# Graph attention on one core: ten of sixteen blocks of a tile turned by DMA instead of eight, with rows grouped by four tiles

## The reference

```python
h = maximum(layernorm(x, axis=-1), 0)             # x: 8192 x 128
scores = einsum('nd,md->nm', h, ks)               # ks: 8192 x 128, so 8192 x 8192 scores
scores = leaky_relu(scores, negative_slope=0.2)
scores = where(adj > 0, scores, -9e15)            # adj: 8192 x 8192 int32
attn = softmax(scores, axis=1)
out = x + einsum('nm,md->nd', attn, ks)
```

## Time and profile before

| | before |
|---|---|
| runs, us | 1636.68, 1636.82, 1636.87 |
| profiled execution, us | 1636.71 |
| its span, first to last instruction, us | 1634.9 |
| busy: PE, PEld, DVE, ACT, POOL | 98%, 72%, 89%, 86%, 71% |
| mean granted TensorE clock | 0.994 |
| HBM read, MB | 276.82 |

### The profile page before, as it was taken

How to read it: one execution, slowest core, us unless ns; L and a number is a source line. 1 busy time by engine, 2 the same in 40 slices (tenths; PEclk the granted TensorE clock), 3 DMA queues, 4 the chain that set the end, 5 groups by cost and what they waited for, 6 DMA issues and landing times.

```text
span 1634.9 us, 38135 instructions
## 1 busy us (share of the span) xinstructions
PE 1599.4 (98%) x13442; PEld 1183.9 (72%) x13442; DVE 1449.5 (89%) x2592; ACT 1401.3 (86%) x2081; POOL 1156.8 (71%) x1224
## 2 busy tenths in 40 slices
PE   5699999999999999999999999999999999999999
PEld 3377777777777777777777777777777777777777
DVE  7989898898898988988998988888898898898986
ACT  6688888888888888888888888888888888888887
POOL 1576776776777777777767777777777767767766
PEclk8999999999999999999999999999999999999999
DMA  7799999999999999999999999999999999999996
GB/s 236 189 232 267 262 269 252 256 274 261 256 266 254 263 266 263 258 261 263 260 271 255 260 271 253 268 266 256 266 265 252 272 261 256 268 254 261 277 256 125
DMA packets 641340, 417.78 MB, mean 256 GB/s; under 512 B 551040, under 2 KB 575616, under 8 KB 641152
## 3 DMA queue, kind: packets, MB, share of 16 engines
q1 hardware_dynamic: 641152, 415.34, 104.7%
HBM read 276.82 MB, written 4.19 MB: 172 GB/s over the span
## 4 chain that ended last, share of the span: by engine, by line
PE 93%; POOL 1%; DVE 0%; ACT 0%; DMA 0%; issue 0%; POOLq 0%; DVEq 0%
PE ps_out L386 26%; PE ps_scores L360 14%; PE ps_out L387 13%; PE ps_T L371 13%; PE ps_scores L362 13%; PE ps_scores L361 13%; POOL keys_in L314 0%; PE ps_out L338 0%; PE ps_out L385 0%; POOL keys_in L312 0%; PE ps_out L384 0%; DMA keys_in<-keys_in 0%; DVE keys L562 0%; DVE mask L573 0%; ACT scores L453 0%
## 5 line engine op out<-in xcount | busy, mean ns | idle before, releaser
L314 POOL TENSOR_TENSOR keys_in<-scores,keys_in 128x512 f16<-128x512 f32 x512 | 652.7, 1275 | 41.4
L591 DVE CUSTOM_DVE_ANT_0 scores<-ps_scores,mask,minus_scale 128x1024 f32<-128x1024 f32 x512 | 654.3, 1278 | 9.7 <-PE ps_scores L362 0.6
L312 POOL CAST keys_in<-scores 128x512 f16<-128x512 f32 x512 | 346.7, 677 | 379.2 <-ACT scores L462 378.9
L462 ACT ACTIVATE scores<-scores,neg_max 128x1024 f32<-128x1024 f32 x512 | 582.7, 1138 | 0.0
L453 ACT ACTIVATE scores<-scores 128x1024 f32<-128x1024 f32 x512 | 537.8, 1050 | 30.6 <-DVE pair_min L591 30.5
L600 DVE TENSOR_TENSOR probsT_lo<-ps_T,probsT_hi 128x512 f16<-128x512 f32 x512 | 352.0, 688 | 142.3 <-ACT probsT_hi L470 142.3
L470 ACT ACTIVATE probsT_hi<-ps_T 128x512 f16<-128x512 f32 x512 | 305.6, 597 | 184.7 <-PE ps_T L371 184.2
L360 PE MATMUL ps_scores<-keysT_hi,hT_hi 128*128 128x512 f16 x1024 | 391.4, 382 | 16.0 <-DVE keysT_lo L555 9.4
L386 PE MATMUL ps_out<-keys,probsT_hi 128*128 128x256 f16 x2048 | 393.6, 273 | 6.7 <-issue 6.0
L361 PE MATMUL ps_scores<-keysT_lo,hT_hi 128*128 128x512 f16 x1024 | 390.9, 382 | 0.0
L362 PE MATMUL ps_scores<-keysT_hi,hT_lo 128*128 128x512 f16 x1024 | 390.4, 381 | 0.0
(11 more groups left out here) (52 smaller groups left out, 831.5 us busy)
## 6 DMA issues: line engine op xcount, KB each, us to landing
adj_in<-in_adj_dram SPq DMA_DIRECT2D x512, 512.0 KB, 5.2
keys_in<-keys_in SPq DMA_TRANSPOSE x512, 5.1
x_in<-in_x_dram SPq DMA_DIRECT2D x64, 64.0 KB, 2.1
keys_in<-in_L_gnn_ks_dram SPq DMA_DIRECT2D x8, 512.0 KB, 7.3
out_dram<-out_tile SPq DMA_DIRECT2D x64, 64.0 KB, 1.8
```

What stands on the lines that cost most here:

```text
L312: nc.gpsimd.tensor_copy(half[:, 0:BLOCK], probs(t, b)).then_inc(half_hi_ready, 1)
L314: nc.gpsimd.tensor_tensor(half[:, BLOCK:2 * BLOCK], probs(t, b), half[:, 0:BLOCK], ALU.subtract) \
L462: nc.scalar.activation(s, s, ACT.Exp, bias=neg_max[:, t % 2:t % 2 + 1], scale=-SLOPE, accum_out=pair_sum[:, t % 2, p:p + 1]).then_inc(prob ...
L591: nc.vector.tensor_tensor_reduce(out=score_pair(q, p), in0=ps_scores[:, slots, :].rearrange("p s k -> p (s k)"), in1=mask[:, (p // 2) % 2, ...
```

## The change

`BY_DMA` gets blocks 4 and 12 as well, so ten blocks of a tile are turned by DMA and six by PE. The slots for halves become 6, for turned blocks 8. Adjacency gets a fourth buffer and is loaded six pairs ahead instead of four. The rows of a group of four tiles are dealt out so that partition p holds rows 4p to 4p+3 of the group: tile s of a group takes every fourth row. With that, one DMA of 256 KB loads `x` for four tiles and one stores four tiles of output, once in four steps; an adjacency row piece is still 4 KB, but the rows of neighbouring partitions lie 128 KB apart instead of 32 KB. On DVE, `split_h` moves from slot 14 to slot 13, ahead of slot 14's `split_probs_lo`, and a tile's first mask moves from slot 0 into slot 14 of the step before (the very first one to the front of the program).

```diff
-    ADJ_SLOTS = 3
+    ADJ_SLOTS = 4
...
-    R_SLOTS = 4
-    X_SLOTS = 4
-    D_SLOTS = 6
+    R_SLOTS = 6
+    GROUP = 4
+    GROUPS = TILES // GROUP
+    D_SLOTS = 8
...
-    BY_DMA = tuple(b for b in range(BLOCKS) if b % 2 == 1)
+    BY_DMA = tuple(b for b in range(BLOCKS) if b % 2 == 1 or b in (4, 12))
...
+        x_groups = x.rearrange("(g p s) d -> g p s d", p=P, s=GROUP)
+        out_groups = out.rearrange("(g p s) d -> g p s d", p=P, s=GROUP)
+        adj_tiles = adj.rearrange("(g p s) m -> g s p m", p=P, s=GROUP)
...
-            def store(t):
-                sp.wait_ge(out_ready, t + 1)
-                sp.dma_start(out[rows(t), :], out_tile[:, :]).then_inc(stored, 16)
+            def store(g):
+                sp.wait_ge(out_ready, (g + 1) * GROUP)
+                sp.dma_start(out_groups[g], out_tile[:, g % 2, :, :]).then_inc(stored, 16)
...
-            for p in range(4):
+            for p in range(6):
                 load_adj(0, p)
...
-                    if j == 11 and prev:
-                        store(i - 1)
-                    if j == 11 and i + 3 < TILES:
-                        load_x(i + 3)
+                    if j == 11 and prev and i % GROUP == 0:
+                        store(i // GROUP - 1)
+                        if i // GROUP + 1 < GROUPS:
+                            load_x(i // GROUP + 1)
...
             find_scales()
+            make_mask(0, 0)
             split_keysT_lo(0)
...
-                    if split and j == 0:
-                        split_probs_lo(*split)
-                    if more and j % 4 == 0:
+                    if more and j in (4, 8, 12):
                         make_mask(i + 1, j // 4)
...
-                    if split and j > 0:
+                    if ahead and j == 13:
+                        split_h(i + 2, odd)
+                    if split:
                         split_probs_lo(*split)
-                    if ahead:
-                        if j == 5:
-                            statistics(i + 2)
-                        if j == 14:
-                            split_h(i + 2, odd)
+                    if ahead and j == 14:
+                        make_mask(i + 2, 0)
+                    if ahead and j == 5:
+                        statistics(i + 2)
```

More of the change, by code:

```diff
@@ L88, in gat_kernel @@
         probsT_lo = sbuf("probsT_lo", [P, T_SLOTS, BLOCK], fp16)
-        x_in = sbuf("x_in", [P, X_SLOTS, D], fp32)
+        x_in = sbuf("x_in", [P, 2, GROUP, D], fp32)
         x_norm = sbuf("x_norm", [P, D], fp32)
@@ L108, in gat_kernel @@
         out_lo = sbuf("out_lo", [P, D], fp32)
-        out_tile = sbuf("out_tile", [P, D], fp32)
+        out_tile = sbuf("out_tile", [P, 2, GROUP, D], fp32)
         ps_scores = psum("ps_scores", [P, SLOTS, BLOCK], fp32)
@@ L118, in gat_kernel @@
         keys_loaded = [sem(f"keys_loaded{p}") for p in range(PAIRS)]
-        x_loaded = [sem(f"x_loaded{s}") for s in range(X_SLOTS)]
+        x_loaded = [sem(f"x_loaded{s}") for s in range(2)]
         stored = sem("stored")
@@ L162, in gat_kernel, with of_tile @@
         SCALED = PAIRS + 8
-        def rows(t):
-            return bass.ds(t * P, P)
+        x_groups = x.rearrange("(g p s) d -> g p s d", p=P, s=GROUP)
+        out_groups = out.rearrange("(g p s) d -> g p s d", p=P, s=GROUP)
+        adj_tiles = adj.rearrange("(g p s) m -> g s p m", p=P, s=GROUP)
+        def of_tile(buffer, t):
+            return buffer[:, t // GROUP % 2, t % GROUP, :]
         def cols(b):
@@ L224, in _, with load_x @@
             key_chunks = ks.rearrange("(c p) d -> p c d", p=P)
[L226 to L229, removed]
-            def store(t):
-                sp.wait_ge(out_ready, t + 1)
-                sp.dma_start(out[rows(t), :], out_tile[:, :]).then_inc(stored, 16)
+            def load_x(g):
+                if g >= 2:
+                    sp.wait_ge(out_ready, (g - 1) * GROUP)
+                sp.dma_start(x_in[:, g % 2, :, :], x_groups[g]).then_inc(x_loaded[g % 2], 16)
+            def store(g):
+                sp.wait_ge(out_ready, (g + 1) * GROUP)
+                sp.dma_start(out_groups[g], out_tile[:, g % 2, :, :]).then_inc(stored, 16)
             def load_adj(q, p):
@@ L239, in load_adj @@
                 sp.dma_start(adj_in[:, n // 2 % ADJ_SLOTS, n % 2 * PAIR:(n % 2 + 1) * PAIR],
-                             adj[rows(q), p * PAIR:(p + 1) * PAIR]).then_inc(adj_loaded[n % (2 * ADJ_SLOTS)], 16)
+                             adj_tiles[q // GROUP, q % GROUP, :, p * PAIR:(p + 1) * PAIR]).then_inc(adj_loaded[n % (2 * ADJ_SLOTS)], 16)
             def turn(t, b):
@@ L262, in step @@
                     if j % 2 == 1:
-                        q, p = divmod((i + 1) * PAIRS + j // 2 + 4, PAIRS)
+                        q, p = divmod((i + 1) * PAIRS + j // 2 + 6, PAIRS)
                         if q < TILES:
@@ L269, in step @@
                             turn(*turning)
-                    if j == 11 and prev:
-                        store(i - 1)
-                    if j == 11 and i + 3 < TILES:
-                        load_x(i + 3)
+                    if j == 11 and prev and i % GROUP == 0:
+                        store(i // GROUP - 1)
+                        if i // GROUP + 1 < GROUPS:
+                            load_x(i // GROUP + 1)
             steps(step)
-            sp.wait_ge(stored, 16 * TILES)
+            sp.wait_ge(stored, 16 * GROUPS)
         @block.gpsimd
@@ L299, in normalise @@
                     pool.wait_ge(hT_done, t)
-                nc.gpsimd.tensor_scalar(x_norm[:, :], x_in[:, t % X_SLOTS, :], mean_var[:, 0:1], rstd[:, 0:1],
+                nc.gpsimd.tensor_scalar(x_norm[:, :], of_tile(x_in, t), mean_var[:, 0:1], rstd[:, 0:1],
                                         ALU.subtract, ALU.mult).then_inc(norm_ready, 1)
@@ L502, in statistics @@
             def statistics(t):
-                dve.wait_ge(x_loaded[t % X_SLOTS], 16 * (t // X_SLOTS + 1))
-                nc.vector.bn_stats(bn[:, :], x_in[:, t % X_SLOTS, :]).then_inc(bn_done, 1)
+                dve.wait_ge(x_loaded[t // GROUP % 2], 16 * (t // GROUP // 2 + 1))
+                nc.vector.bn_stats(bn[:, :], of_tile(x_in, t)).then_inc(bn_done, 1)
                 dve.wait_ge(bn_done, t + 1)
@@ L634, in finish @@
                 nc.vector.scalar_tensor_tensor(out=out_lo[:, :], in0=ps_out[:, odd, 0:D], scalar=weight[:, 0:1],
-                                               in1=x_in[:, t % X_SLOTS, :], op0=ALU.mult, op1=ALU.add).then_inc(lo_scaled, 1)
+                                               in1=of_tile(x_in, t), op0=ALU.mult, op1=ALU.add).then_inc(lo_scaled, 1)
                 dve.wait_ge(lo_scaled, t + 1)
-                if t > 0:
-                    dve.wait_ge(stored, 16 * t)
-                nc.vector.scalar_tensor_tensor(out=out_tile[:, :], in0=ps_out[:, odd, D:2 * D], scalar=weight[:, 0:1],
+                if t >= 2 * GROUP:
+                    dve.wait_ge(stored, 16 * (t // GROUP - 1))
+                nc.vector.scalar_tensor_tensor(out=of_tile(out_tile, t), in0=ps_out[:, odd, D:2 * D], scalar=weight[:, 0:1],
                                                in1=out_lo[:, :], op0=ALU.mult, op1=ALU.add).then_inc(out_ready, 1)
```

## The result

Four runs of the changed kernel gave 1704.95 to 1708.58 us, median 1705.26; the kernel before gave 1636.75 beside them. The ratio is 1.042, 95% interval 1.041 to 1.044. The forecast was 1586, faster. The profiled execution took 1704.95 us, its span 1703.1.

The account below looks back on a forecast made before the run. PE was taken to set the pace. From 1636.7 us: -61.4 for PE, -0.5 at the start, +5 at the end, +6 for small collisions, nothing for the DMAs, giving 1586 us; range 1573 to 1616.

Parts of the forecast that it names:

- What PE loses: PE's step drops eight transposes (0.86 us) and a 0.13 us hole: 24.68 to 23.69 us, 61.4 us over 62 steps.
- What the DMAs gain: DMA queue and SP: 7.0 MB per step at 295 GB/s fits, taken as nothing, bounds -0.05 and +0.05 us per step.
- I put no cost on it: Two more turns per step on the DMAs cost nothing: slices reach 367 GB/s and PE hardly ever waited for a turn.
- No wait of PE: Argument against a full queue: PE waited for a block turned by DMA only once, 0.3 us.
- SP's sum: SP's issues per step, 10 turns and 8 loads: 16.9 to 26.9 us, 21.9 taken, fits with little left.
- the DMA queue is full already: Rival: queue gives only 262 GB/s, step 26.7 us, about 1760 us; chance 0.07 slower, 0.10 for 284 to 295 GB/s.
- Its threshold: DMA queue: below a sustained 284 GB/s the change loses; between 284 and 295 it wins less.
- Its sign: For the full queue: landing times well over 5.1 us while POOL still waits.
- POOL becomes the bound: Rival: dearer collisions with DVE's masks make POOL's step 23.9 to 24.0 us, time 1598 us; chance 0.25.
- POOL's own step: POOL with ten halves: 21.5 us of work plus two more mask collisions, 23.4 us, 0.3 us under PE's step.
- The sign that I gave for this rival: POOL without idle time, and PE waiting for DMAs of `keys_in` by 0.2 us a step or more.
- Start and end: Start: mask -1 us, larger `x` load +0.5; end: POOL's last tile and larger store +5 us, bounds 2 and 8.

Follow-up runs that it names:

- e16: Changed kernel with adjacency loads after the first four buffers cut to an eighth, and POOL's halves of blocks 4 and 12 to 16 of 512 columns: 1575.52 us.
- e10: Changed kernel with eight turned blocks, and two 512 KB adjacency loads that nobody reads where blocks 4 and 12 would be turned: 1627.67 us.
- e4: Changed kernel, ten blocks turned, each adjacency load after the first four buffers moving only an eighth of its columns: 1612.27 us.
- e13: Changed kernel with eight turned blocks, and two turns of keys that nobody reads where blocks 4 and 12 would be turned: 1710.61 us.
- e2: Changed kernel, ten blocks turned, with the adjacency loads issued by ACT on a queue of their own: 2170.54 to 2249.62 us.
- e1: Changed kernel with only the eight odd blocks turned, as before; the rest of the change stays: 1628.13 us, ratio 0.995.

## Why the prediction was wrong, step by step

**What PE loses: right.** The transposes fell from 2048 to 1536, the hole closed, and PE's step without other limits is 23.66 us (`e16`); I had 23.69.

**What the DMAs gain: this step failed.** "I put no cost on it" rested on three readings.
- I priced the turns by bytes: 7.0 MB in place of 6.5, 8% more. By the fitted prices the queue's step goes from 22.3 to 25.8 us, 16% more: a turn of 256 KB costs 1.8 loads of 512 KB. The trace of before could have warned of it. Its packets' durations from 300 to 1500 us, shared out over the 16 engines, are 1.69 us per turn and 1.54 per load; ten turns, eight loads and the 0.7 us of the rest in 23.69 us are a share of 1.26, against 1.08 then. No run here passes 1.15 in a steady stretch of one queue. As a price these durations fail, though: they give `e10` a share of 1.21, and it lost nothing, since a load's packets took only 1.39 us there.
- I read the slices of 339 to 367 GB/s as reserve and the dips to 107 as pauses. The row above those slices, the engines' busy share in tenths (a packet counts whole in the slice in which it starts), I left out:

```profile
DMA  9999995899999999699989999869999999987999
```

The dip to 138 GB/s (second slice) has a 9: a turn's packets held the engines there, 1024 of 256 B beside 16 of 4 KB, and some of them stood still for 1.4 us (last section). The dip to 107 has an 8 and is a turn as well. Only some dips are pauses. The same two rows after the change, in the same stretch:

```profile
DMA  9999999996999999999998999997999999999999
GB/s 350 133 341 256 292 288 226 361 238 185 359 303 279 280 241 96 361 252 311 214 178 269 349 288 231 298 249 247 344 233 229 306 270 141 297 245 302 284 287 228
```

- "No wait of PE" says only that turns came in time, with a queue that needed 22.3 of 24.67 us, not that there was room for two more.

SP's sum was of the right size (21.9 us taken; 10 x 1.91 + 8 x 0.62 = 24.1 measured, more than the forecast step), but a turn's issue time is no constant of SP's: with the same list it was 1.33 us in `e4`, so what is above that is the queue's answer.

**The rival "the DMA queue is full already": right in kind**, and given 0.07. Its threshold held (269 GB/s sustained, under the 284 below which the change loses), its time of 1760 was too high: a fixed rate in bytes was the wrong measure, as 305 and 328 GB/s show. Its sign failed as well: landing did not go "well over 5.1 us". The delay stands between half and issue instead.

**The rival "POOL becomes the bound": a second part, hidden by the first.** Without the queue's limit the time is 1612 us, 37 above `e16`; I had 1598, from a sum that writes 3 x 1.08 where it names 1.04 (with 1.04 the step is 23.8 us, hardly above PE's). POOL's own step of 23.4 us was 0.9 too long (371.0 of 400 us at 24.25 us a step is 22.5). The sign that I gave for this rival, PE waiting for DMAs of `keys_in`, came from the queue: POOL still waited 150.3 us for exponentials. What I missed is the other side: I let POOL alone pay for a collision, while a busier POOL also stops DVE, whose list stands between a mask and PE's next operand. The rule of the Trainium skill ("SBUF — State Buffer", Who interferes with whom) that the later of the two waits says both; here DVE's mask went to 2.12 us, from 1.22 in the earlier trace rows.

**Start and end: right.** The tail behind the last tile's first score product grew by 3.1 us (5 forecast, 2 to 8), and the third tile's first score product comes at 80.61 us, 80.66 before.

**The sum.** From `e16` to the changed kernel: 1575.5, + 37 for POOL and DVE's masks (`e4`), + 93 for the queue. The order matters: in `e13` POOL makes only eight halves and the time is no shorter than the changed kernel's, so while the queue sets the pace POOL's part costs nothing. The two prices are fitted, not measured one by one, and why a turn is so dear is only partly open to view (last section).

## What to carry to other kernels

Before work is moved to DMAs, do not price it by bytes, and read GB/s only beside the busy share of the same slices. The time that the packets of each kind take on the engines is a warning, not a price. A queue that no one waits for may have no room; add idle DMAs of the kind in question and see when the first wait appears. When a step has two candidates to move, move one, and try either: nine blocks won 2% with block 12 and 0.5% with block 4, ten lost 4%.

## What the runs showed of the hardware

**The engines stop inside a turn.** DMA busy tenths and GB/s of the changed kernel from 802 to 805 us, 40 slices of 75 ns (a slice counts the packets that start in it, so a 0 is no idle engine):

```profile
DMA  7999999596599999990000000000000100799909
GB/s 222 399 253 430 219 229 178 123 345 119 119 229 256 266 198 75 51 14 0 0 0 0 0 7 7 7 10 7 10 10 7 14 7 10 157 290 434 749 0 874
```

Packets of 256 B take 18 ns each (median); then, from 803.1 to 804.6, 19 of them take 1.3 to 1.5 us and end within 0.03 us of each other, while hardly anything else moves. Time above 18 ns, shared out over the 16 engines, is some 0.45 us per turn in this kernel, 0.54 before. Part of it falls together with the loading of instructions: from 300 to 1500 us, 58 such stops (12 packets of 256 B or more, each over 0.2 us, that end together) last over 1.2 us, and 47 of them overlap a 16 KB packet of the instruction queue (q8 on the page), as this one does (802.60 to 803.78); of the 145 shorter stops 4 do. That the one holds the other up was not tried, and what the shorter stops wait for the trace doesn't show. The Trainium skill ("DMA: Bandwidth & Descriptors", Latency and other measured facts) gives 261 GB/s for a transposing DMA with a non-contiguous middle dimension; by that 256 KB would take an estimated 1.0 us. The slices of 229 to 266 GB/s above agree; the fitted 1.76 us (149 GB/s) for a turn among loads does not.

**A second queue made it worse.** In the trace of `e2` the turns' issue grew from 1.91 to 3.09 us on average and the rate fell to 207 GB/s. The loads slowed as well: they landed in 8.3 us, 5.3 in the changed kernel. The Trainium skill ("DMA: Bandwidth & Descriptors", Queues, rings and completion order) says that an engine takes turns between the queues that have work for it, a whole packet of several descriptors at a time. The two queues did share the 16 engines here, with 66.5% and 48.7% of their time; why both came out slower no run shows.

**Larger packets didn't help.** 1 MB loads (8 KB packets) moved 254 GB/s where 512 KB loads moved 269, and the turns' issue grew: 3.81 us on average (2.59 to 5.23) for a turn that is the second behind a load, 2.29 in the changed kernel. A pitch of 128 KB between rows costs nothing visible: loads landed in 5.0 us in `e1`, 5.2 before with 32 KB.
